# B products of the Mamba scan: eight units by scaled du and transposes in place of six by diagonals, and fifteen C products on GpSimd

## What is computed

```python
xz = einsum('bld,ed->ble', layernorm(x), in_proj_w); x, z = split(xz)     # 512 + 512 channels
u = silu(causal depthwise conv of x, width 4, + conv_b)
dt_lo, B, C = split(u @ x_proj_w.T)                                       # 64, 16, 16
delta = softplus(dt_lo @ dt_proj_w.T + dt_proj_b)
h_t = exp(delta_t * A) * h_{t-1} + (delta_t * u_t) * B_t                  # 512 channels x 16 states
y_t = sum over states of h_t * C_t
out = ((y + u * D) * silu(z)) @ out_proj_w.T
```

## Time and profile before

| | us |
|---|---|
| median of 3 runs (lowest, highest) | 3346.77 (3342.35, 3348.41) |
| span of the profiled execution, first to last instruction | 3323.2 |
| Mamba stage, first scan to last C product | 96 to 1790 |

### The profile page before, as it was taken

One profiled execution on the slowest core, in us unless ns is written; L12 is line 12 of the kernel. 1 busy time (PEld: TensorE's weight loads), 2 busy tenths in 40 slices (PEclk: granted clock), 3 DMA queues, 4 the chain that ended last, 5 costly groups with the idle time before them and its releaser, 6 DMA issues.

```text
span 3323.2 us, 54121 instructions
## 1 busy us (share of the span) xinstructions
PE 2699.6 (81%) x20202; PEld 1494.4 (45%) x20202; DVE 2305.5 (69%) x2483; ACT 1719.1 (52%) x3115; POOL 2124.3 (64%) x1317
## 2 busy tenths in 40 slices
PE   5787788877888788887864299996999999269998
PEld 2233333433333334333332156664676777235665
DVE  1799999999999999999996632211666676542211
ACT  3677777777777777777763022222444443022222
POOL 1899999999999999999994035533333333024543
PEclk9899999988998889988976599998999999579999
DMA  3556556665566565665561124432111111213442
GB/s 112 106 128 148 140 140 135 152 142 134 122 147 153 140 141 136 141 147 141 132 130 65 22 58 90 90 58 56 40 46 53 53 46 40 67 34 83 90 90 26
DMA packets 227392, 330.02 MB, mean 99 GB/s; under 512 B 40545, under 2 KB 116833, under 8 KB 227010
## 3 DMA queue, kind: packets, MB, share of 16 engines
q1 hardware_dynamic: 202562, 292.49, 35.8%
q0 software_dynamic: 24576, 34.10, 6.1%
HBM read 240.52 MB, written 85.98 MB: 98 GB/s over the span
## 4 chain that ended last, share of the span: by engine, by line
PE 44%; POOL 25%; DVE 20%; issue 7%; ACT 3%; DMA 2%; SPq 0%; DVEq 0%; POOLq 0%; ACTq 0%
POOL m_side L584 15%; PE t_wb L2062 8%; POOL m_hc L593 7%; DVE m_pair L668 7%; PE f_h L1341 6%; PE g_h L1341 6%; DVE m_hc L668 5%; PE m_wk L771 3%; PE f_yp L1355 3%; PE g_yp L1355 3%; PE t_num L2062 2%; DVE m_hc L677 2%; PE t_a_ps L2062 2%; PE m_y L863 2%; PE m_pair L919 2%
## 5 line engine op out<-in xcount | busy, mean ns | idle before, releaser
L584 POOL TENSOR_TENSOR m_side<-m_du_r,m_bc 128x1024 f32<-128x1024 f32 x416 | 975.0, 2368 | 13.2 <-DMA m_du_r<-ddd 13.0
L351 ACT ACTIVATE m_pair<-m_delta_r,m_a_neg 128x512 f32<-128x512 f32 x832 | 539.7, 681 | 179.1 <-DVE m_hc L677 128.7
L593 POOL TENSOR_TENSOR m_hc<-m_hc,m_bc 128x1024 f32<-128x1024 f32 x208 | 492.3, 2370 | 99.4 <-DVE m_hc L668 97.7
L668 DVE TENSOR_TENSOR_SCAN m_pair<-m_pair,m_side 128x1024 f32<-128x1024 f32 x240 | 548.0, 2283 | 3.3 <-ACT m_pair L351 2.8
L863 PE MATMUL m_y<-m_hc,m_fold 128*32 128x512 f32 x2048 | 322.1, 703 | 229.4 <-DVE m_hc L677 120.9
L668 DVE TENSOR_TENSOR_SCAN m_hc<-m_pair,m_side 128x1024 f32<-128x1024 f32 x176 | 397.8, 2275 | 28.5 <-ACT m_pair L351 28.5
L677 DVE TENSOR_TENSOR m_hc<-m_pair,m_bc 128x1024 f32<-128x1024 f32 x304 | 370.5, 1219 | 7.3
L771 PE MATMUL m_wk<-m_xnT,m_w_in 128*128 128x512 f32 x512 | 276.1, 666 | 10.7 <-DVE m_cw_diag L725 9.8
L771 PE MATMUL m_wk<-m_xs,m_cw_diag 128*128 128x512 f32 x512 | 244.1, 605 | 15.5 <-ACT m_xs L416 15.5
L919 PE MATMUL m_pair<-m_b_diag,m_du_t 128*32 128x128 f32 x6144 | 203.6, 289 | 44.0 <-DVE m_hc L668 24.4
L919 PEld LDWEIGHTS m_pair<-m_b_diag,m_du_t 128*32 128x32 f32 x6144 | 178.8, 117 | 125.1 <-issue 123.7
(11 more groups left out here) (308 smaller groups left out, 4884.8 us busy)
## 6 DMA issues: line engine op xcount, KB each, us to landing
m_delta_r<-ddd SPq DMA_DIRECT2D x256, 256.0 KB, 6.8
m_du_r<-ddd SPq DMA_DIRECT2D x256, 256.0 KB, 7.7
m_bc<-bcd SPq DMA_DIRECT2D x256, 128.0 KB, 3.0
ddd<-m_delta SPq DMA_DIRECT2D x32, 512.0 KB, 3.2
ddd<-m_du SPq DMA_DIRECT2D x32, 512.0 KB, 4.2
f_w<-in_w SPq DMA_DIRECT2D x24, 512.0 KB, 6.2
g_w<-in_w SPq DMA_DIRECT2D x24, 512.0 KB, 6.1
m_xt<-in_x SPq DMA_DIRECT2D x16, 512.0 KB, 10.7
```

What stands on the lines that cost most here:

```text
L351: last = nc.scalar.activation(to, delta_r[:, c % 2, q, :], ACT.Exp, scale=a_neg[:, c * NQ + q, st:st + 1])
L584: nc.gpsimd.tensor_tensor(side[:, un % RING, :, :], du_r[:, c % 2, 2 * h:2 * h + 2, :], bc[:, 0, st:st + 1, :].to_broadcast([P, 2, T]), AL ...
L593: nc.gpsimd.tensor_tensor(hc[:, un % RING, :, :], hc[:, un % RING, :, :], bc[:, 1, st:st + 1, :].to_broadcast([P, 2, T]), ALU.mult).then_i ...
L668: nc.vector.tensor_tensor_scan(to, decay, added, 0.0, ALU.mult, ALU.add).then_inc(S["scan"], 1)
```

## The change

Units get another order of sets (`ORDER`, `SET[un]`; groups and halves stay), so that all products of set 3 are PE's. `ON_PE` becomes (4, 7, 10, 13, 22, 23, 27, 30) and `ON_POOL` 15 units in place of 13. POOL makes 24 B products in place of 26, DVE 17 C products in place of 19.

PE no longer multiplies with diagonals: ACT scales the transposed du of two groups at once by B (`scaled`, 4 activations of 128x256 a step, 8 steps a batch, into `prod`), and PE transposes the result back into `pair` (8 transposes a unit). `load_bc` leaves out the B half of set 3. `dut(3)` moves on PE from slot 18 to 11 and its copy on ACT from slot 18 to 12; `btr` moves on PE from slot 12 to 13.

```diff
-ON_POOL = (0, 3, 4, 8, 9, 12, 13, 16, 18, 21, 24, 27, 28)
-ON_PE = (2, 15, 18, 22, 27, 31)
+BY_PE = 3
+ORDER = (((0, 0), (0, 1), (1, 0), (1, 1), (3, 0), (2, 1), (2, 0), (3, 1)),
+         ((0, 0), (0, 1), (3, 0), (1, 1), (1, 0), (3, 1), (2, 0), (2, 1)),
+         ((0, 0), (0, 1), (1, 0), (1, 1), (2, 0), (2, 1), (3, 0), (3, 1)),
+         ((0, 0), (0, 1), (1, 0), (3, 1), (2, 0), (1, 1), (3, 0), (2, 1)))
+SET = [st for units in ORDER for st, _ in units]
+ON_POOL = (0, 2, 4, 5, 7, 8, 10, 11, 13, 16, 20, 22, 24, 26, 28)
+ON_PE = tuple(un for un in range(UN) if SET[un] == BY_PE)
...
+            def scaled(b, g, n):
                 if n == 0:
                     act.wait_ge(S["b_t"], b + 1)
+                    act.wait_ge(S["du_t"], b * 4 + 2 * g + 2)
+                    if g:
+                        act.wait_ge(S["dBp"], b * NE_ + E_LAST[0])
+                    elif not below(b, 1):
+                        act.wait_ge(S["dBp"], b * NE_)
                 for k in range(TJ):
-                    last = nc.scalar.activation(b_diag[:, i, n, k, :], ident[:], ACT.Identity,
-                                                scale=b_t[:, k, PE_SETS[i] * NL + n:PE_SETS[i] * NL + n + 1])
+                    last = nc.scalar.activation(prod[:, :, :, k, n * SB:(n + 1) * SB],
+                                                du_t[:, k, :, :].rearrange("p c (h f d) -> p (c h) f d", h=2, d=SB),
+                                                ACT.Identity, scale=b_t[:, b % 2, k, BY_PE * NL + n:BY_PE * NL + n + 1])
...
-                for i in range(len(PE_SETS)):
-                    for n in range(NL):
-                        diag(0, i, n)
...
                 dut_out(0, 1)
+                scaled(0, 0, 0)
...
-                    if post and un + UN in (27, 30, 31, 32, 33, 34, 35, 36):
-                        diag(b, (27, 30, 31, 32, 33, 34, 35, 36).index(un + UN) // NL, ...)
+                    if un < 3:
+                        scaled(b, 0, un + 1)
...
+                    if un == 12:
+                        dut_out(b, 3)
+                    if un in (14, 18, 19, 20):
+                        scaled(b, 1, (14, 18, 19, 20).index(un))
...
                             dut_out(b + 1, 0)
                             dut_out(b + 1, 1)
+                            scaled(b + 1, 0, 0)
...
                 if un in E_FIRST:
-                    wait_alone(pe, S["du_t"], b * 4 + c + 1, S["tick"])
+                    wait_alone(pe, S["pr"], b * 2 + c // 2 + 1, S["tick"])
                 for f in range(2):
-                    q = 2 * h + f
                     for k in range(TJ):
-                        for n in range(NL):
-                            last = nc.tensor.matmul(pair[n * SB:(n + 1) * SB, un % 2, f * T + k * P:f * T + (k + 1) * P],
-                                                    du_t[:, c % 2, k, q * SB:(q + 1) * SB], b_diag[:, i, n, k, :],
-                                                    start=True, stop=True, skip_group_check=True)
+                        last = nc.tensor.transpose(pair[:, un % 2, f * T + k * P:f * T + (k + 1) * P],
+                                                   prod[:, c % 2 * 2 + h, f, k, :], ident[:])
```

More of the change, by code:

```diff
@@ L55 @@
 NE_, NG_ = E_BEFORE[UN], G_BEFORE[UN]
-E_FIRST = [min(un for un in ON_PE if un // 8 == c) for c in range(4)]
+E_FIRST = [min(un for un in ON_PE if un // 16 == g) for g in range(2)]
+E_LAST = [E_BEFORE[16], NE_]
 G_FIRST = [min(un for un in range(8 * c, 8 * c + 8) if un not in ON_PE) for c in range(4)]
-LAST_OF = [E_BEFORE[1 + max(un for un in ON_PE if un % 8 // 2 == st)] for st in PE_SETS]
+LAST_OF = [1 + max(un for un in range(UN) if SET[un] == st) for st in range(NSET)]
 RESET = 1e30
@@ L193, in mamba @@
                  "ab ex sp de du dz "
-                 "btr b_t dut du_t dg0 dg1 dA dBu dBp scan hD hP sum yg op x1 bs1 agg1 ve1 rstd1 nm1 xn1 pt ptev scm scev").split()
+                 "btr b_t dut du_t pr dA dBu dBp scan hD hP sum yg op x1 bs1 agg1 ve1 rstd1 nm1 xn1 pt ptev scm scev").split()
         S = {n: s.sem(n) for n in names}
@@ L243, in load_bc @@
                 if not below(b, 1):
-                    last = UN - 2 * (NSET - st) + 2
+                    last = LAST_OF[st]
                     wait_alone(sp_, S["dBu"], (b - 1) * NG_ + G_BEFORE[last], S["tick"])
@@ L248, in load_bc @@
                 src = bcd.rearrange("(k s n) t -> s n k t", k=2, n=NL)
+                first = 1 if st == BY_PE else 0
                 for n in range(NL):
-                    sp_.dma_start(bc[n * SB:(n + 1) * SB, :, st, :], src[st, n].partition_broadcast(SB))\
+                    sp_.dma_start(bc[n * SB:(n + 1) * SB, first:, st, :], src[st, n, first:].partition_broadcast(SB))\
                         .then_inc(S[f"ld_bc{st}"], 16)
@@ L813, in iz @@
                     pe.wait_ge(S["izev"], b * 4 + dt - 1)
-                elif below(b, 1):
-                    pe.wait_ge(S["de"], 4)
                 else:
-                    pe.wait_ge(S["du_t"], b * 4)
+                    pe.wait_ge(S["de"], b * 4 + 4)
                 for k in range(KC):
@@ L871, in btr @@
                 wait_alone(pe, S["xdev"], b + 1, S["tick"])
-                if below(b, 2):
+                if below(b, 1):
                     wait_alone(pe, S["cvev"], b * 4 + 4, S["tick"])
                 else:
-                    wait_alone(pe, S["x1"], b * 2 - 2, S["tick"])
+                    wait_alone(pe, S["du_t"], b * 4, S["tick"])
                 for k in range(TJ):
@@ L894, in dut @@
                         pe.wait_ge(S["du_t"], b * 4 + 1)
-                elif prep:
-                    pe.wait_ge(S["de"], b * 4 + 8)
+                elif below(b, 1):
+                    pe.wait_ge(S["cvev"], 8)
                 else:
@@ L1010, in body @@
                             xp(b + 1, 1 - par, (11, 12).index(un))
-                        if un == 12:
-                            btr(b + 1)
+                    if un == 11:
+                        dut(b, 3, post, prep)
+                    if prep:
                         if un in (12, 15, 16, 17):
                             dtp(b + 1, (12, 15, 16, 17).index(un))
-                    if un == 18:
-                        dut(b, 3, post, prep)
+                        if un == 13:
+                            btr(b + 1)
                     if prep and un in (18, 20, 21, 25):
```

43 lines of the change are left out of this document (16 added, 27 removed).

## The result

The changed kernel takes 3460.35 us (median of 4 runs, 3458.42 to 3462.54), the kernel before 3345.29 in the same comparison: ratio 1.0342, 95% interval 1.0329 to 1.0355, some 115 us slower. The forecast was 3424, its range 3366 to 3466.

The account below looks back on a forecast made before the run. DVE bounds the kernel by share, with PE full in slots 1 to 9. Fourteen batches +82, batch 0 +1 and the prologue -5.4 give +77.6 on the median 3346.8: 3424 us, range 3366 to 3466.

Parts of the forecast that it names:

- main step: Slots 1 to 9: PE's in-order queue holds products 4, 7 and 10 behind the next batch's preparation, so scan 10 waits.
- Scan 10 starts at 37.45: Slot 10, counted from scan 0: DVE ready at about 32.6, so 4.9 us idle for PE's B product 10.
- Scan 4 ... starts at 15.0: Slot 4, counted from scan 0: due at 13.2, 1.9 us late because B product 4 stands behind conv(1).
- Slots 10 to 31 ... 74.5: Rest of a batch from scan 10: 74.7 us today, 73.0 after savings, 74.5 with new lateness; period 112.0.
- late products 27 and 30: Late in a batch, B products 27 and 30 lose a spare 1.27 us and come some 0.35 late each.
- exp 2 ... 1.15 us late: ACT at the batch's head: exp 2 ends at 6.8 against due 5.65, behind ix(1)'s copy and scaling; now 1.05 late.
- My rival on the clock: PE's full stretch: 4 us of it at half speed, scan 10 4 us later, 3480 us; chance 0.04.
- PE's queue binds, the waits don't: Slots 1 to 10: scaling at the low end, slack absorbs late products; scan 10 at 35.0, period 108.0, 3368 us; chance 0.15.
- bound of 35.0 for scan 10: PE's work from the fold to product 10, 31.65 plus three products of 1.05 and 0.2 latency, waits not counted.
- walk to 37.45: Slots 0 to 10: ACT's and PE's lists followed with their waits, B product 10 ending at 37.4.
- Faster: PE reaches B product 10 by 28.8, so DVE and POOL bound: period 103.7, 3305 us; chance 0.05.
- All of it dearer: Scaling at 2.2 a step, products 27 and 30 0.8 dearer at low clock: period 115.1, 3469 us; chance 0.13.

## Why the prediction was right, and where it was off

**Right in the main step.** "Scan 10 starts at 37.45": 37.57 in batch 8, 38.12 in the mean. "Scan 4 ... starts at 15.0": 15.10 and 15.65. Both outp stand ahead of product 10, the residual and scan 10 wait 4.92 together where 4.9 was said. A share of 79% for PE over a steady stretch said nothing of this; the window over slots 1 to 9 did. The time is right less closely: +115 measured against +77.6, 6 us inside the upper end of the range.

**Sizes.** A transpose product takes 1.04, said 1.05; a scaling activation 495 ns, said 0.49; the Trainium skill's "ScalarE: Activation LUTs", What ACT_TABLE_LOAD costs, would have given 492, and the trace agrees with it. DVE's work fell by 2.0 a batch, said 2.5.

**The term that was too small** is "Slots 10 to 31 ... 74.5": measured 75.9 in batch 8 (1114.92 - 1039.05). I let delta's wait stay at 1.1, having looked at slot 17 alone. In slot 15 a new wait of 1.65 stands. POOL's list looks like its cause, since unit 15 was PE's and is now POOL's. These are B products 14 and 15 and then C product 13 of the changed kernel, and C products 12 and 13 of the kernel before:

```profile
1047.80 4.71 POOL L594 TENSOR_TENSOR m_side<-m_du_r,m_bc 128x1024 f32<-128x1024 f32 x2
1052.44 2.36 POOL L603 TENSOR_TENSOR m_hc<-m_hc,m_bc 128x1024 f32<-128x1024 f32 x1
...
988.99 4.71 POOL L593 TENSOR_TENSOR m_hc<-m_hc,m_bc 128x1024 f32<-128x1024 f32 x2
```

But C product 12 went to DVE, and counted from scan 10 C product 13 ends no later than before, at 15.75 us against 16.33. The fold that waits for it starts at 15.90 against 16.47. What differs is PE's speed. These are the fold and the two dtp of slots 15 and 16 in the kernel before:

```profile
993.84 1.07 PE L863 MATMUL m_y<-m_hc,m_fold 128*32 128x512 f32 x8 [0.50 <-POOL m_hc L593]
994.84 1.98 PE L771 MATMUL m_wk<-m_xd,m_w_dt 97*128 97x512 f32 x4
```

In the changed kernel the same two rows take 1.93 and 3.78, in every batch, behind a gap of 5.53 (before: product 15 and a gap of 0.50); from 1055 to 1061 the granted clock is 0.50, that is 1.2 GHz. ACT's softplus, which waits for the first dtp, ends at 21.79 after scan 10 (before 20.55), and DVE, which has less to do, is there at 20.26 (before 21.90). An estimate: at the lengths of before, the fold would have been 0.86 and the first dtp 0.9 shorter, and the softplus done at 20.0, in time. So the forecast missed a gap that a removed product opens on PE and the clock behind it. dtp ahead of the fold removed the wait. The late products 27 and 30, on the other hand, didn't come (0.7 said, 0 measured).

**The second** is the low clock at the head of every other batch: "exp 2 ... 1.15 us late" holds for batch 8 (1.20), the mean is 1.75. My rival on the clock had it inside slots 4 to 10, where the clock stayed at 1.00 in batch 8.

**Sum.** Batches 1 to 14 cost 14 x 8.17 = +114.3 (said 82), batch 0 +1.5 (said 1), batch 15 -1.5 (said 0), the first scan came 2.4 us earlier (said 5.4): POOL's first product set it, as forecast, but the work ahead of it came about 3 us later in this execution than in the one of before. Sum +111.9, measured 115. In the other kernels of this study with the new form, whose work up to there is the same, the first scan stands anywhere between 91.25 and 94.26. The 23.6 us by which the median stood above the span were no time around the span: in the changed kernel the two are 3.8 apart, and the profiled execution of before was the quicker one behind the stage. Adding the change to the median was right all the same.

**Rivals.** "PE's queue binds, the waits don't" fell: the waits of ACT's chain came. Its bound of 35.0 for scan 10 was too low as well: PE's fold starts 0.75 us after scan 0 (946.76 against 946.01), from which all times are counted, so that the same sum gives 35.8. The walk to 37.45 doesn't use it. "Faster" fell with PE's queue (the terms that it names, 28.8 + 73.0 + 2.7, give 104.5 and not 103.7). "All of it dearer" gave 3469, nearest to the measured time, but by causes that weren't these: scaling did not cost 2.2 a step.

**What is shown, and what isn't.** That PE's queue holds product 10 back is shown: with outp(1) behind it, scan 10 came 3.7 us earlier and its wait was gone. That this is the whole price of the change is not: the period fell by 1.5 only, and without products 4 and 10 a loss of 4.8 of 8.2 stayed. The waits of the table add up to the loss (12.80 - 2.65 of new waits, less 2.0 of work); but they cover one another, so that none of them is worth its size.

**Whether it can be mended.** Six of the kernels move work around within the changed one; none beats the kernel before. With eight products DVE's own work is 101 a batch, so under 5 us of waits are allowed, and each move let another list's wait show: ACT's silu block, the residuals behind outp, POOL at unit 19. A plan that moves outp, its residuals and the silu block together wasn't tried.

## What to carry to other kernels

Where engines run fixed lists in order, a product is worth what it costs at its place: sum the list of its engine from the last forced start to it, and compare with when the consumer is due. An engine at 79% over a period can be full in one third of it. And when a wait is removed, look for what was hidden under it before counting the gain; here a wait of 3.63 us hid one of 2.74.

## What was not expected of the hardware

PE's low clock followed small shifts in time: a move that took work away from ahead of a gap made iz(2) run 3.78 instead of 1.98 us and cost more than it saved; and in the changed kernel the clock fell at the head of every second batch, at the same list and behind the same gap of 1.93 us.

With the same program, the median of the kernel before also moved from 3345 to 3325 us between comparisons, more than the spread within one (at most 9 us). The traces show where: behind the Mamba stage, in code that is the same in all kernels, the profiled executions took 1547 to 1553 us in the comparisons in which the kernel before stood at 3345 and 3337, and 1529 to 1533 in those in which it stood at 3325; the profiled execution of the kernel before, 1531, is of the second kind. Between the changed kernel and the kernel before, half of it lies in the first and half in the second layer of experts; why stays open.
